# A new opening for a two-layer adapter kernel: the first four row tiles come from transposed column tiles, loads on two queues, out(0) by chunk, orders written anew

## The reference

```python
# L0: adapter, residual, layer norm
h = relu(x @ W1[id0] + b1[id0])             # 512 -> 128
v = x + h @ W2[id0] + b2[id0]               # 128 -> 512
n = (v - mean(v)) * rsqrt(var(v) + 1e-5)
x = x + n * gamma[id0] + beta[id0]
# L1
return x + x @ W[id1] + b[id1]              # 512 -> 512
```

## Time and profile before

| | us |
|---|---|
| median of 3 runs | 313.61 |
| lowest, highest run | 313.02, 1758.34 |
| span of the profiled execution | 312.3 |
| PE busy in it | 303.9 |
| DVE, ACT, POOL busy | 225.6, 211.1, 225.8 |

### The profile page before, as it was taken

One profiled execution on the slowest core, in us unless ns is written; L12 is line 12 of the kernel. 1 busy time (PEld: TensorE's weight loads), 2 busy tenths in 40 slices (PEclk: granted clock), 3 DMA queues, 4 the chain that ended last, 5 costly groups with the idle time before them and its releaser, 6 DMA issues.

```text
span 312.3 us, 4810 instructions
## 1 busy us (share of the span) xinstructions
PE 303.9 (97%) x1424; PEld 244.4 (78%) x1424; DVE 225.6 (72%) x641; ACT 211.1 (68%) x381; POOL 225.8 (72%) x185
## 2 busy tenths in 40 slices
PE   8988999999999999999999999999999999999995
PEld 8424678888888888888888888888888888888884
DVE  0185989696986869598686969778695977889610
ACT  1045667886696958778596857958686874857431
POOL 0649685999779995999959996899959995541000
PEclk9999999999999999999999999999999999999999
DMA  6999795778766798768867888677867381111122
GB/s 199 338 364 370 237 338 176 218 233 284 216 172 212 207 297 250 182 185 258 275 192 197 232 256 247 154 215 246 303 202 198 111 300 37 67 67 71 67 101 101
DMA packets 40943, 65.39 MB, mean 209 GB/s; under 512 B 6100, under 2 KB 10196, under 8 KB 40916
## 3 DMA queue, kind: packets, MB, share of 16 engines
q1 hardware_dynamic: 40336, 64.03, 66.2%
q10 hardware_dynamic: 580, 1.05, 1.1%
HBM read 48.29 MB, written 16.78 MB: 208 GB/s over the span
## 4 chain that ended last, share of the span: by engine, by line
PE 92%; DVE 4%; ACT 2%; issue 1%; POOL 0%; POOLq 0%
PE out_ps L778 54%; PE down_ps L778 14%; PE h_ps L778 13%; PE turn_ps L833 9%; PE turn_ps L904 2%; DVE y L488 1%; ACT y L376 1%; DVE stats L493 1%; DVE turn_ps L532 0%; DVE x1T_lo L539 0%; ACT w_hi L347 0%; ACT hT L358 0%; ACT out_sb L394 0%; DVE mean_var L497 0%; ACT w_hi L341 0%
## 5 line engine op out<-in xcount | busy, mean ns | idle before, releaser
L778 PE MATMUL out_ps<-x1T_hi,w_hi 128*128 128x512 f32 x256 | 100.4, 392 | 0.0
L778 PE MATMUL out_ps<-x1T_lo,w_hi 128*128 128x512 f32 x256 | 99.8, 390 | 0.0
L778 PE MATMUL out_ps<-x1T_hi,w_lo 128*128 128x512 f32 x256 | 99.7, 389 | 0.0
L687 POOL TENSOR_TENSOR xrow<-xrow,b_rows 128x512 f32<-128x512 f32 x64 | 82.6, 1294 | 9.3 <-DMA xrow<-x_rows 9.3
L385 ACT ACTIVATE x1T_hi<-turn_ps,gamma_beta 128x512 fp32r<-128x512 f32 x64 | 43.2, 689 | 43.7 <-DVE turn_ps L532 43.7
L532 DVE SCALAR_TENSOR_TENSOR turn_ps<-turn_ps,gamma_beta,xT 128x512 f32<-128x512 f32 x64 | 45.4, 754 | 34.4 <-PE turn_ps L833 33.5
L376 ACT ACTIVATE y<-y,shift,rstd 128x512 f32<-128x512 f32 x64 | 52.2, 818 | 20.4 <-DVE shift L523 20.0
L692 POOL TENSOR_TENSOR xT_lo<-xT,xT_hi 128x512 fp32r<-128x512 f32 x48 | 62.4, 1300 | 4.7 <-ACT xT_hi L328 4.7
L488 DVE TENSOR_TENSOR y<-down_ps,xrow 128x512 f32<-128x512 f32 x64 | 43.7, 683 | 19.6 <-PE down_ps L778 19.5
L778 PEld LDWEIGHTS out_ps<-x1T_hi,w_hi 128*128 128x128 f32 x256 | 48.1, 188 | 10.9 <-issue 0.8
L778 PEld LDWEIGHTS out_ps<-x1T_hi,w_lo 128*128 128x128 f32 x256 | 48.1, 188 | 10.1 <-issue 0.2
(11 more groups left out here) (40 smaller groups left out, 356.8 us busy)
## 6 DMA issues: line engine op xcount, KB each, us to landing
xrow<-x_rows SPq DMA_DIRECT2D x32, 512.0 KB, 6.7
out_cols<-out_sb SPq DMA_DIRECT2D x64, 256.0 KB, 2.6
xT<-x_cols SPq DMA_DIRECT2D x30, 512.0 KB, 6.2
w<-w_all SPq DMA_DIRECT2D x8, 1024.0 KB, 7.2
w<-w_all SPq DMA_DIRECT2D x15, 256.0 KB, 5.2
b_rows<-b_all SPq DMA_DIRECT2D x8, 256.0 KB, 8.1
xT<-x_cols ACTq DMA_DIRECT2D x4, 256.0 KB, 4.6
w<-w_all SPq DMA_DIRECT2D x4, 64.0 KB, 3.7
```

Of the source, the lines that this page charges most:

```text
L687: nc.gpsimd.tensor_tensor(xrow[:, i % XR, :], xrow[:, i % XR, :], b2_rows[:, m % 2, :], ALU.add).then_inc(rowbias_done, 1)
L778: mm = nc.tensor.matmul(out, lhsT, rhs, start=first and n == 0, stop=last and n == len(terms) - 1)
```

## The change

- **The sums of the first four row tiles.** `seed(k)` transposes the four blocks of column tile k on PE into the four sum banks: `down_ps[0]`, `down_ps[1]`, `out_ps[0]`, `out_ps[1]` (`sum_bank`). down(0..3) then add h @ W2 to what lies there. `add_bias(i)` on DVE adds b2 to the bank in place of `bias_rows` and `add_rows`; rows 0 to 3 are not loaded. b2 of the first sample has a semaphore of its own.
- **Two queues.** ACT issues also cols 4 (behind the table load), cols 6 (behind relu(0)) and rows 4 (behind w_high(0, 0)). SP's list is in a new order.
- **out by chunk.** `out_part(i, k)` waits only for x1_low of its chunk k and, at the first tile of a sample, for w_low(m, k). out(0), out(1), out(2), out(4) and out(6) are begun by chunk, with downs and ups between.
- **Banks.** turn(2) uses `out_ps[1]`, turn(3) uses `turn_ps[0]` (`turn_bank`).
- **Orders.** `opening()` is written anew on all five engines and reaches to `OPEN` = 15. 12 warm-ups in place of 20. The tiles with plain products are the same (16 ups, 8 downs), now written by block.

```diff
+    SEEDED = BLOCK
-    OPEN = 11
-    WARM_UPS = 20
+    OPEN = 15
+        def sum_bank(i):
+            return out_ps[i - 2] if 2 <= i < SEEDED else down_ps[i % 2]
+        def turn_bank(i):
+            return {2: out_ps[1], 3: turn_ps[0]}.get(i, turn_ps[i % 2])
...
             def load_w1(m):
-                if 2 <= m < 4:
-                    sp.wait_ge(up_done, PER * (m - 1))
+                if m >= 2:
+                    sp.wait_ge(up_done, min(PER * (m - 1), PLAIN_UP))
```

SP's opening list, as far as cols 12 (the rest of the new one: rows 8, b2(1), rows 10, w2(2), cols 14, 16, 18, w(1), b(1), rows 12, 14, w1(3), store(0), b2(2), rows 16, stores 1 and 2, and so on to store(6)):

```diff
                 load_first_w1(0)
                 load_first_w1(1)
-                load_b1(0)
-                load_b2(0)
                 load_first_w1(2)
                 load_first_w1(3)
-                load_rows(0)
+                load_first_b2()
                 load_w2(0)
-                load_rows(2)
+                load_b1(0)
                 load_w(0)
-                load_cols(4)
                 load_w1(1)
-                load_cols(6)
+                load_cols(sp, nc.sync, 8)
+                load_cols(sp, nc.sync, 10)
+                load_gamma_beta(0)
                 load_w2(1)
-                load_cols(8)
-                load_rows(4)
+                load_w1(2)
+                load_rows(sp, nc.sync, 6)
                 load_b(0)
-                load_gamma_beta(0)
-                load_cols(10)
-                load_rows(6)
-                load_cols(12)
                 load_b1(1)
-                load_w1(2)
+                load_cols(sp, nc.sync, 12)
```

ACT's opening list, to the first x1_high:

```diff
-                for k in range(KC):
-                    load_first_cols(k)
+                load_first_cols(0)
+                load_first_cols(1)
                 load_ids()
+                load_first_cols(2)
+                load_first_cols(3)
                 load_table()
+                load_cols(act, nc.scalar, 4)
                 relu(0)
+                load_cols(act, nc.scalar, 6)
                 standard(0)
+                w_high(0, 0)
+                load_rows(act, nc.scalar, 4)
                 standard(1)
                 standard(2)
-                w_high(0, 0)
+                relu(1)
+                standard(3)
                 normalise(0)
-                w_high(0, 1)
-                standard(3)
-                w_high(0, 2)
                 normalise(1)
                 normalise(2)
+                normalise(3)
+                w_high(0, 1)
+                w1_high(2)
+                w_high(0, 2)
+                x1_high(0)
+                w_high(0, 3)
                 w2_high(1)
-                normalise(3)
-                relu(1)
-                x1_high(0)
                 x1_high(1)
```

DVE, the first sums, and its opening list behind mean_shift(3):

```diff
+            def add_bias(i):
+                dve.wait_ge(down_done, i + 1)
+                if i == 0:
+                    dve.wait_ge(b2_first_in, 16)
+                nc.vector.tensor_tensor(y[:, i, :], sum_bank(i)[:], b2_rows[:, 0, :], ALU.add).then_inc(y_done, 1)
...
+                add_rows(4)
+                add_rows(5)
                 merge(0)
                 merge(1)
-                add_rows(4)
+                statistics(4)
                 x1_low(0)
+                merge(2)
                 x1_low(1)
```

POOL's opening list, to h_low(2) (behind it: bias_rows(9), x_lo(16), bias_rows(10), bias_rows(11), w_diagonal(1), x_lo(17), bias_rows(12), w1_low(2), x_lo(18), h_low(3), ...):

```diff
-                bias_rows(0)
-                bias_rows(1)
-                bias_rows(2)
-                bias_rows(3)
                 w_diagonal(0)
                 w_low(0, 0)
+                bias_rows(4)
+                bias_rows(5)
                 w_low(0, 1)
                 w_low(0, 2)
-                bias_rows(4)
-                bias_rows(5)
+                w_low(0, 3)
+                w2_low(1)
                 bias_rows(6)
-                w_low(0, 3)
                 bias_rows(7)
+                bias_rows(8)
                 h_low(2)
```

PE's new and changed functions:

```diff
+            def seed(k):
+                wait_cols(pe, k)
+                for i in range(SEEDED):
+                    nc.tensor.matmul(sum_bank(i)[:, k * P:(k + 1) * P], xT[:, k, i * P:(i + 1) * P], ident[:],
+                                     start=k == 0, stop=False, is_transpose=True, skip_group_check=True)
...
             def down(i):
-                if i >= 2:
-                    pe.wait_ge(y_done, i - 1)
+                if i >= SEEDED:
+                    pe.wait_ge(y_done, i - 1 if i >= SEEDED + 2 else i + 1 - SEEDED)
...
-            def out(i):
+            def out_part(i, k):
                 if i % PER == 0:
-                    pe.wait_ge(wlo_done, KC * (m + 1))
+                    pe.wait_ge(wlo_done, KC * m + k + 1)
                 if j == 0:
-                    pe.wait_ge(x1lo_done, BLOCK * (blk + 1))
+                    pe.wait_ge(x1lo_done, BLOCK * blk + k + 1)
```

More of the change, by code:

```diff
@@ L304, in _ @@
             opening()
-            for s in range(4, LAST + 1):
+            for s in range(OPEN, LAST + 1):
                 step(s)
@@ L613, in opening @@
                 merge(4)
+                mean_variance(9)
                 merge(5)
-                statistics(9)
                 x1_low(4)
+                x1_low(5)
                 rstd_start(8)
-                mean_variance(9)
-                x1_low(5)
+                rstd_start(9)
                 rstd_newton(8)
+                add_rows(10)
+                add_rows(11)
+                merge(6)
+                statistics(10)
+                statistics(11)
+                rstd_newton(9)
@@ new lines, in opening @@
+                rstd_newton(10)
+                add_rows(12)
+                rstd_start(11)
+                rstd_newton(11)
+                statistics(12)
+                rstd_end(10)
+                rstd_end(11)
+                x1_low(7)
+                add_rows(13)
+                mean_shift(10)
+                mean_shift(11)
+                mean_variance(12)
+                statistics(13)
+                rstd_start(12)
+                mean_variance(13)
+                merge(8)
@@ new lines, in opening @@
+                merge(9)
+                rstd_newton(12)
+                x1_low(8)
+                x1_low(9)
+                add_rows(14)
+                statistics(14)
+                merge(10)
+                mean_variance(14)
+                merge(11)
+                rstd_start(13)
+                rstd_newton(13)
+                rstd_end(12)
+                rstd_end(13)
+                x1_low(10)
+                x1_low(11)
+                mean_shift(12)
+                mean_shift(13)
@@ L775, in _, with product, warm_up @@
         def _(pe):
-            def product(out, terms, first=True, last=True):
+            def product(out, terms, first=True, last=True, unchecked=False):
                 for n, (lhsT, rhs) in enumerate(terms):
                     mm = nc.tensor.matmul(out, lhsT, rhs, start=first and n == 0,
-                                          stop=last and n == len(terms) - 1)
+                                          stop=last and n == len(terms) - 1, skip_group_check=unchecked)
                 return mm
+            def warm_up(n):
+                for _ in range(n):
+                    nc.tensor.matmul(turn_ps[0][:, :P], ident[:], ident[:], start=True, stop=True)
             def up(i):
@@ L822, in down @@
                     terms = [(hi, w2_hi[:, m % 2]), (hi, w2_lo[:, m % 2]), (lo, w2_hi[:, m % 2])]
-                product(down_ps[i % 2][:], terms).then_inc(down_done, 1)
+                product(sum_bank(i)[:], terms, first=i >= SEEDED, unchecked=i < SEEDED).then_inc(down_done, 1)
             def turn(i):
@@ new lines, in out_part, with out @@
+                x1 = (blk * BLOCK + k) % WR
+                return product(out_ps[i % 2][:], [(hi, x1T_hi[:, x1]), (lo, x1T_hi[:, x1]), (hi, x1T_lo[:, x1])],
+                               first=k == 0, last=k == KC - 1)
+            def out(i):
+                for k in range(KC - 1):
+                    out_part(i, k)
+                out_part(i, KC - 1).then_inc(out_done, 1)
+            def opening():
+                seed(0)
+                up(0)
+                up(1)
+                up(2)
+                up(3)
+                seed(1)
+                seed(2)
+                seed(3)
@@ L902, in _ @@
             pe.wait_ge(ident_done, 1)
-            for _ in range(WARM_UPS):
-                nc.tensor.matmul(turn_ps[0][:, :P], ident[:], ident[:], start=True, stop=True)
+            warm_up(12)
             opening()
```

341 lines of the change are left out of this document (216 added, 125 removed).

## The result

| kernel | median us | lowest, highest | ratio to before, 95% interval |
|---|---|---|---|
| before | 313.81 (20 runs) | 313.02, 1758.34 | |
| changed | 312.66 (20 runs) | 311.21, 313.98 | 0.9965 [0.9954, 0.9977] |

The change makes the kernel 1.15 us faster at the median, 0.35%. The median lies inside the range of the prediction, but 4.1 us were forecast, and the gain is a quarter of that.

What follows compares the result with a forecast made beforehand. PE bounds the kernel, its opening latency and loads. Start 7.05 + work 55.1 + seeds 1.31 + idle 0.5, 0.7, 0.9 puts step(15) at 65.6 against 69.65, 4.1 us less: median 309.5 us, range 307.4 to 313.2.

Steps and rivals of the forecast that it cites:

- The sum of work: Products and turns from up(0) to step(15): 55.1 us of PE work, plus 1.31 for seeds.
- the waits: PE idle before step(15): 0.5 us ahead of turn(0), 0.7 at down(8), 0.9 for the reshuffled rest.
- The second queue: Opening loads: ACT's cols 4 there by 10 to 11, cols 6 at 16.5; total bandwidth unchanged, only the order improves.
- a sign of being wrong: Profile after: PE waiting over 1 us for xT or for ACT's x1T_hi would show the prediction wrong.
- the second queue brings nothing: Rival, chance 0.12: columns of up(6) land at 21.0, turn(0) at 27.0, 3.2 later, giving 312.7 us.
- The waits inside SP: SP's waits for stores and slots hold only loads used at least 8 us later, so they cost nothing.
- The seeds: Twelve seed transposes behind up(3) cost 1.31 us of PE time, to 11.8.
- The start: With 12 warm-ups, up(0) starts at 7.05 instead of 8.91, 1.86 us earlier.
- down(8): Needs h_low(2), behind POOL's additions, done at 35.3; PE comes at 34.6 and waits 0.7 us.
- The offset: Median run time 313.61 stands 1.3 us above the profiled span; added to span 308.2 it gives 309.5.
- The clock rival: Chance 0.10: warm-ups end before PE is fast, first four ups run at half speed, cost 3.4 us; 312.9.
- slower: Rival, chance 0.06: w1_high(2) waits on ACT for w1(2) ahead of x1_high(0); landing at 31.1 gives 315.2 us.

Runs made afterwards that it cites:

- the kernel with one queue and both b1 moves: Changed kernel with cols 4, cols 6, rows 4 issued by SP, b1(0) ahead of b2 and w2(0), b1(2) behind b1(1): 309.23 us, ratio 0.9857.
- the second run of one queue: The kernel with both b1 moves and cols 4, cols 6, rows 4 on SP, measured once more unchanged: 309.12 us, ratio 0.9851.
- out begun as a whole: Against the kernel with both b1 moves, one queue and cols 12 ahead of w1(2): each out waits for all four chunks' x1_low and w_low; 316.19 us.

## Why the prediction was right or wrong

**The frame held.** PE bounds the kernel, all is decided ahead of `step(15)`, the steady steps and the end are unchanged (206.40 of 206.40 us busy after). The sum of work, 55.1 + 1.31, was right to 0.7 us: in the kernel with one queue and both b1 moves `step(15)` begins at 64.75, where it gives 64.0 from up(0)'s true start near 7.6, without any idle. What failed are the waits. Their sum was also added up wrong: the prediction's own times leave 0.8 ahead of turn(0) (23.8 less 7.05, 17 x 0.86 and 1.31), where it took 0.5.

**The second queue** ("with nothing of its queue but 1.05 MB ahead", "I take 16.5") is the step that failed most. I asked what the second queue does for cols 4 and cols 6 and not what it takes from w1 and b1(0). w1 landed in 4.7 to 5.4 us and not in about 4; b1(0) landed at 11 to 13.1, not "by 11"; cols 6 took 7.65 us where 4.6 were assumed, and landed at 19.1, between my 16.5 and the bound of 21.0. PE waited 1.3 us for them, over the 1 us that the prediction named as a sign of being wrong. Moving the three loads to SP gives 2.1 us; that the sharing does it, and not the earlier issue of cols 4, is argued from the landings of w1. The rival "the second queue brings nothing" had the right place and a chance of 0.12; it ends at 312.7, near the measured median, but by luck: it has turn(0) at 27.0, which stood at 25.45 and 26.6, and no loss at the urgent loads or at b1(2).

**b1(0)** was moved from ahead of two w1 pieces to behind b2 and w2(0). I gave it a landing in half a sentence, with no margin against relu(0), which releases down(0) and the issue of cols 6. It is about 0.7 us with the second queue; with one, b1(0) was in time in its new place and in its old.

**The waits inside SP** ("hold loads used at least 8 us later, so nothing") failed as well. b1(2) stands behind three stores, was issued at 49.5 and used at 53, and costs 0.9 us. Cols 12, behind w1(2) and its wait for up(7), were issued at 23.4 and 24.6 and wanted 6 us later. I hadn't put a time of issue beside each load's time of use. The queue, b1(0) and b1(2) moved together bring 3.4 us, and the forecast had missed the median by 3.1.

**The seeds** were charged 1.31 and cost nothing that the runs of the changed kernel show. **The start** was credited with 1.86 and brings about 0.7. The two errors nearly cancel. up(0) began at 7.67 in the first profile, when w1's first piece was in (7.53). But 7.05 wasn't to be had every time with an earlier w1 either: in the second run of one queue it was in by 7.0, and up(0) began at 7.64, since the warm-ups ended at 7.02 and not 6.65 and seed(0), behind them, took 0.6 and not 0.4.

**down(8)** was given 0.7 us of wait, and has none to 0.3 in the profiles; **out by chunk** had the times right (the first chunk at 28.9 with one queue, as forecast).

**The offset** of 1.3 us between span and run took a long execution for a median one; with the 1.77 seen since, the median before stands for a span of 312.0.

**The clock rival** fell: the weight loads of the first ups take 0.19 us each in the profile after, as in before behind its warm-ups, and four ups take 3.79 with a wait inside. The seeds between warm-ups and up(0) did no harm, so the rule of the Trainium skill (TensorE: Matmul & The Clock Gate, "Part 4: PE-mode transpose"), that transposes don't count as PE-busy for the clock, changed nothing here; four transposes are too few to try it. The first half of the rival's premise was right: in seven of the twelve profiles with 12 warm-ups and seeds the weight loads of the last warm-ups were still slow, 0.27 us or more. The rival *slower*, w1(2), fell: it landed 2.7 us after its issue at 21.3.

## What to carry to other kernels

When a second queue is added, ask first which small, urgent loads its transfers will run beside: in a stretch where the DMA engines are full, it adds no bandwidth, and 64 KB on the path of everything can pay for 512 KB that had time. Put every load's issue, as the lists of its engine give it, beside the first use of what it brings, small ones (a bias of 128 numbers behind a store) above all. And look at where the profiled execution lies among the others before reading it as the typical one: the two profiles of the changed kernel were near its shortest and at its longest, with other waits in each. An idle time of PE can cost more than itself: look at the granted clock behind it.

## What the runs showed of the hardware

A load of 128 numbers, b1(0) on SP, took from issue to landing: ahead of b2 and w2(0), 2.5 to 3.2 us with one queue and 4.5 to 5.5 with 512 KB or more on ACT's queue beside it; behind them, 4.2 with one queue and 4.9 to 7.0 with two, 4.9 and 6.9 of these in two executions of the same kernel. From 8.9 to 20 us the DMA engines moved 343 to 360 GB/s with both queues in use and 340 to 363 with one.

The granted clock of TensorE stayed at 1.00 behind an idle time of 2.6 us and was 0.51 for 3.2 us behind one of 2.8, in one execution (out begun as a whole). Over the six executions of that kernel a mean granted clock of 1.000 went with 314.79 us and one of 0.988 with 317.98. At the start of the kernel PE's weight loads went from 333 to 192 ns at a moment that differs between executions: before 4.9 us in one, not before 6.4 in others, though all began the same warm-ups at 1.53.
